# Vision transformer block with mixture of experts, one core: clock-holding products moved from the attention steps to the stretch before the token tiles, exp(min(x,0)) taken straight from PSUM, late weights loaded later

## What is computed

```python
h = concat([cls_tok, concat([cls_token, patches @ W_emb + b_emb]) + pos_embedding])
q, k, v = split(layernorm(h) @ qkv_w.T)          # 12 heads of 16
fmap(x) = elu(x) + 1                              # max(x, 0) + exp(min(x, 0))
out = wl * local_band(q, k, v, window 12) + ws * stride_band(q, k, v, 3) + wg * global_band(q, k, v, 12 anchors)
h = h + out @ out_w.T
xs = layernorm(h); topv, topi = top_k(softmax(xs @ Wg), 2); cw = topv / sum(topv)
h = h + sum over the 2 choices of cw * (relu(xs @ W1[e] + b1[e]) @ W2[e] + b2[e])     # 8 experts, 192 -> 768 -> 192
```

## Time and profile before

| | us |
|---|---|
| three runs | 254.42, 254.91, 259.94 (median 254.91) |
| the profiled execution | 253.24, of which its span is 251.3 |
| PE busy in the span | 226.0 (90%) |
| DVE, ACT, POOL busy | 141.4, 111.2, 71.6 |
| mean granted TensorE clock | 0.971 of full speed |

### The profile page before, as it was taken

The page is one execution under the profiler, slowest core; times in us unless marked ns, Lnnn a source line. Parts: engine busy times, 40 slices in busy tenths (PEclk is TensorE's granted clock), DMA queues, the critical chain, the costliest instruction groups (busy, mean ns, idle before and its releaser), DMA issues.

```text
span 251.3 us, 5038 instructions
## 1 busy us (share of the span) xinstructions
PE 226.0 (90%) x1662; PEld 193.5 (77%) x1662; DVE 141.4 (56%) x422; ACT 111.2 (44%) x253; POOL 71.6 (28%) x87
## 2 busy tenths in 40 slices
PE   8979998898999999999989839879999999999930
PEld 8968896675777757676878719679999999999930
DVE  5353588696859578574656790557867324334100
ACT  2364847753323744535086870345334344243210
POOL 4013160832040502213036610003324224233240
PEclk9999999999999999999999956999999999999996
DMA  6999999999500000001014945522423323322213
GB/s 129 199 239 160 232 265 267 301 259 265 194 4 0 3 1 4 0 0 31 0 32 144 329 95 132 118 78 49 73 40 57 55 37 60 54 39 18 28 18 90
DMA packets 26261, 25.78 MB, mean 103 GB/s; under 512 B 4970, under 2 KB 23261, under 8 KB 26221
## 3 DMA queue, kind: packets, MB, share of 16 engines
q1 hardware_dynamic: 22333, 22.17, 35.3%
q0 software_dynamic: 3568, 2.64, 7.9%
q10 hardware_dynamic: 336, 0.66, 1.5%
HBM read 16.57 MB, written 7.77 MB: 97 GB/s over the span
## 4 chain that ended last, share of the span: by engine, by line
PE 66%; DVE 10%; DMA 9%; ACT 7%; issue 4%; SPq 1%; POOL 1%; another core or an unknown queue 0%; DVEq 0%; POOLq 0%; ACTq 0%
PE ps L1025 11%; PE ps L1002 11%; PE ps L825 6%; PE ps L738 6%; PE ps L567 5%; DMA sums<-ys,xs 5%; DMA wemb<-in_L_tok_W_emb 4%; PE ps L1014 3%; PE ps L598 3%; PE ps L701 3%; PE ps L572 2%; PE ps L734 2%; PE ps L811 2%; ACT w1hi L1573 1%; ACT w1hi L1574 1%
## 5 line engine op out<-in xcount | busy, mean ns | idle before, releaser
L1765 POOL DMA_INDIRECT sums<-ys,xs x17 | 26.3, 1546 | 73.5 <-ACT ys L1652 66.8
L1025 PE MATMUL ps<-w2s,hidT 128*128 x204 | 36.1, 327 | 1.1 <-DVE hidT L1448 0.8
L567 PE MATMUL ps<-ones 114*128 114x128 f32 x238 | 34.8, 301 | 1.1 <-DVE ones L1073 1.1
L1025 PEld LDWEIGHTS ps<-w2s,hidT 128*128 128x128 f32 x204 | 33.1, 189 | 2.1 <-issue 1.6
L567 PEld LDWEIGHTS ps<-ones 114*128 114x128 f32 x238 | 32.1, 213 | 2.1 <-DVE ones L1073 1.1
L1002 PE MATMUL ps<-w1hi,xhi 128*128 x68 | 24.4, 359 | 2.6 <-issue 1.3
L1427 DVE TENSOR_TENSOR xlo<-ps,xhi 128x128 fp32r<-128x128 f32 x17 | 5.0, 292 | 35.8 <-ACT xend L1645 35.8
L1652 ACT ACTIVATE ys<-ps,xs 128x192 f32<-128x192 f32 x17 | 7.2, 421 | 39.9 <-PE ps L1025 37.6
L1534 ACT ACTIVATE qlb<-ps,cst 96x228 f32<-96x228 f32 (+1 forms) x36 | 12.1, 425 | 17.2 <-PE ps L772 17.1
L825 PE MATMUL ps<-qlb,kT 96*114 96x342 f32 (+1 forms) x48 | 18.0, 457 | 1.7 <-DVE at L1219 1.1
L1219 DVE TENSOR_TENSOR at<-ps,cst 114x342 f32<-114x342 f32 (+1 forms) x24 | 11.3, 471 | 8.7 <-PE ps L825 8.3
(11 more groups left out here) (202 smaller groups left out, 462.5 us busy)
## 6 DMA issues: line engine op xcount, KB each, us to landing
w2s<-in_L_ffn_W SPq DMA_DIRECT2D x8, 576.0 KB
sent<-blank SPq DMA_DIRECT2D x1, 3977.0 KB, 31.6
w1s<-in_L_ffn_W SPq DMA_DIRECT2D x4, 768.0 KB, 17.2
xs<-sent SPq DMA_DIRECT2D x17, 96.0 KB, 2.0
w1s<-in_L_ffn_W SPq DMA_DIRECT2D x4, 384.0 KB, 18.6
w1hi<-w1hi SPq DMA_DIRECT2D x8, 192.0 KB, 3.0
ximg<-in_x SPq DMA_DIRECT2D x12, 96.0 KB, 7.8
w1s<-in_L_ffn_b SPq DMA_DIRECT2D x1, 792.0 KB
```

What stands on the lines that cost most here:

```text
L567: pe.matmul(bank[:, 0:128], ones[:], ones[:], start=True, stop=True)
L1025: last = pe.matmul(ps[6 + j % 2][:, 0:D], hidT[:, k, :], of_expert(w2s[:, :, k, :], expert), start=(k == 0), stop=(k == FCH - 1))
L1765: po.indirect_dma_start(sums, bass.IndirectOffsetOnAxis(ap=xs[:, j % NS, D + TAIL + 1:].bitcast(U32), axis=0), ys[:, j % 2, :], None, comp ...
```

## The change

1. *Feature map.* A row of ones is added to the turned, normalised tokens (`xhT`) and to the query and key columns of the turned weights (`wT`), so that the projection gives x + 1 in the same two matmuls (97 rows in place of 96 in the first). ACT takes exp(x + 1 - 1) from PSUM, with the bias tile `minus`; DVE makes min(max(x + 1, 1), exp(x)), which is the same function. `qkmin` and its step on DVE go. Three small memsets are added at DVE's start.
2. *Products of ones.* In the steps, the 3 asides at `m` 1 and 3 stay in step 3 alone; 3 asides are put ahead of `through_anchors` in steps 6 and 7. Step 8 is as before. Of steps 9 and 10 the ones of the first part of step 9 stay; 1, 1 and 2 in step 9, 8 and 1 in step 10 and the 6 behind it go. Behind the counts stand 4; then, in place of 3 and 26, there are 4 once ACT has rounded 3 experts, 5 once it has rounded 5, 5 once it has rounded 6, and 6 once all scatters have landed.
3. *Late W2.* The loads of experts 4 to 7 move behind the stores of `first` on SP's queue, with a semaphore of their own (`w2_late`), for which PE waits at tile 5; at tile 1 it waits for experts 0 to 3 alone.
4. *ACT.* `combine_out(1)` moves ahead of the rounding of experts 4 and 5. `tokens_high` signals after its first instruction; the second (`xend`) reads the SBUF result of the first and has a semaphore of its own.
5. *DVE.* The six sums `first` come ahead of `tokens_low(0)` and `tokens_low(1)`.
6. *PE at the tiles.* Four register loads stand ahead of the first tile. The five products of a half are reordered, so that those that need `xend` and `xlo` come later, each with its own wait; `turn_tokens(1)` goes between the two halves of tile 0.

```diff
@@ SP
-                sp.dma_start(w2s[:, e], w2[e]...).then_inc(w2_in, 16)
+                sp.dma_start(w2s[:, e], w2[e]...).then_inc(w2_in if e < AHEAD else w2_late, 16)
...
             attention_over(sp)
-            for e in range(AHEAD, E):
-                load_w2(e)
...
                 sp.dma_start(sums[t0:t0 + n, :], first[0:n, g, :]).then_inc(sums_in, 16)
+            for e in range(AHEAD, E):
+                load_w2(e)
@@ PE, project_qkv
                 for i in range(2):
+                    rows = HALF + 1 - i
-                    last = pe.matmul(ps[2][0:n, 0:2 * D], xhT[:, i, t0:t0 + n], wT[:, i, 0:2 * D],
+                    last = pe.matmul(ps[2][0:n, 0:2 * D], xhT[0:rows, i, t0:t0 + n], wT[0:rows, i, 0:2 * D],
@@ PE, the steps
                 if 0 <= t - 3 < GROUPS:
+                    if GROUPS <= t < GROUPS + 2:
+                        hold_clock_aside(ps[5], 3)
                     through_anchors(t - 3)
...
-                        elif t < GROUPS + 2:
+                        elif t == 3:
                             hold_clock_aside(ps[5], 3)
...
-                    if m == 2 and t == GROUPS + 4:
-                        hold_clock(ps[3], 8)
...
-                if t >= GROUPS + 3:
-                    hold_clock(ps[3], 1)
                 if 0 <= t - 5 < GROUPS:
                     logits(t - 5)
-                if t == GROUPS + 3:
-                    hold_clock(ps[3], 1)
...
                 if t == GROUPS + 3:
-                    hold_clock(ps[3], 2)
                     places(GROUPS - 2)
...
-            hold_clock(ps[3], 6)
             places(GROUPS - 1)
...
+            hold_clock(ps[3], 4)
             output_biases(range(4))
             turn_combine(range(4, GROUPS))
-            hold_clock(ps[3], 3)
+            pe.wait_ge(ac_w1_high, 3)
+            hold_clock(ps[3], 4)
             output_biases(range(4, GROUPS))
-            hold_clock(ps[3], 26)
+            for e in (4, 5):
+                pe.wait_ge(ac_w1_high, e + 1)
+                hold_clock(ps[3], 5)
+            pe.wait_ge(sent_in, 16 * TOP * GROUPS)
+            hold_clock(ps[3], 6)
@@ PE, the tiles
+            for j in range(FIXED):
+                experts[j] = pe.value_load(own[0:1, j:j + 1], min_val=0, max_val=E - 1)
             pe.wait_ge(dv_count, 1)
             turn_tokens(0)
-            turn_tokens(1)
...
-                    hidden(j, experts[j])
+                    hidden(j, experts[j], 0)
+                    if j == 0:
+                        turn_tokens(1)
+                    hidden(j, experts[j], 1)
                 if j == 1:
-                    pe.wait_ge(w2_in, 16 * E)
+                    pe.wait_ge(w2_in, 16 * AHEAD)
+                if j == AHEAD + 1:
+                    pe.wait_ge(w2_late, 16 * (E - AHEAD))
@@ DVE, features
-                ve.tensor_scalar(qkmin[0:n, :], src, 0.0, None, ALU.min).then_inc(dv_min, 1)
...
-                link(ve.scalar_tensor_tensor(qtok[0:n, g % 2, :], src[:, 0:D], 0.0, qkexp[0:n, 0:D], ALU.max, ALU.add))
+                link(ve.scalar_tensor_tensor(qtok[0:n, g % 2, :], src[:, 0:D], 1.0, qkexp[0:n, 0:D], ALU.max, ALU.min))
@@ DVE, ahead of the tiles
+            for g in range(GROUPS):
+                first_sum(g)
             tokens_low(0)
             tokens_low(1)
-            for g in range(GROUPS):
...
@@ ACT
-                    ac.wait_ge(dv_min, t + 1)
+                    ac.wait_ge(pe_qk, t + 1)
...
-                    ac.activation(qkexp[0:n, :], qkmin[0:n, :], ACT.Exp).then_inc(ac_exp, 1)
+                    ac.activation(qkexp[0:n, :], ps[2][0:n, 0:2 * D], ACT.Exp, bias=minus[0:n, :]).then_inc(ac_exp, 1)
...
             weights_high(3)
+            combine_out(1)
             weights_high(4)
...
             weights_high(5)
-            combine_out(1)
```

More of the change, by code:

```diff
@@ L74 @@
 NS = 6
+FIXED = 4
 EPS_LN = 1e-5
@@ L233, in build @@
         sb = pool(attn)
-        qkmin = sb("qkmin", [GTOK, 2 * D])
         qkexp = sb("qkexp", [GTOK, 2 * D])
@@ L704, in project_qkv @@
                 for i in range(2):
-                    last = pe.matmul(ps[3][0:n, 0:D], xhT[:, i, t0:t0 + n], wT[:, i, 2 * D:3 * D],
+                    last = pe.matmul(ps[3][0:n, 0:D], xhT[0:HALF, i, t0:t0 + n], wT[0:HALF, i, 2 * D:3 * D],
                                      start=(i == 0), stop=(i == 1))
@@ L986, in of_expert, with hidden @@
                 return weights[:, bass.ds(expert, 1)].rearrange("p e f -> p (e f)")
-            def hidden(j, expert):
-                pe.wait_ge(ac_x_high, j + 1)
-                pe.wait_ge(dv_x_low, j + 1)
-                for c in range(2):
-                    if j >= 1:
-                        pe.wait_ge(dv_hidden if c else ac_hidden, j)
-                    cols = slice(c * PASS, (c + 1) * PASS)
-                    products = ((xhi[:, j % 2, 0, :], w1hi[:, :, 0, cols]),
-                                (xlo[:, j % 2, :], w1hi[:, :, 0, cols]),
-                                (xhi[:, j % 2, 0, :], w1lo[:, :, 0, cols]),
-                                (xhi[:, j % 2, 1, :], w1hi[:, :, 1, cols]),
-                                (xend[:, j % 2, :], w1lo[0:END, :, 1, cols]))
-                    for n, (xx, ww) in enumerate(products):
-                        last = pe.matmul(ps[2 + c][:, 0:PASS], xx, of_expert(ww, expert),
-                                         start=(n == 0), stop=(n == len(products) - 1))
-                    last.then_inc(pe_hidden, 1)
+            def hidden(j, expert, c):
+                if c == 0:
+                    pe.wait_ge(ac_x_high, j + 1)
+                if j >= 1:
+                    pe.wait_ge(dv_hidden if c else ac_hidden, j)
+                cols = slice(c * PASS, (c + 1) * PASS)
+                products = ((xhi[:, j % 2, 0, :], w1hi[:, :, 0, cols]),
+                            (xhi[:, j % 2, 0, :], w1lo[:, :, 0, cols]),
+                            (xend[:, j % 2, :], w1lo[0:END, :, 1, cols]),
+                            (xlo[:, j % 2, :], w1hi[:, :, 0, cols]),
+                            (xhi[:, j % 2, 1, :], w1hi[:, :, 1, cols]))
+                for n, (xx, ww) in enumerate(products):
+                    if c == 0 and n == 2:
+                        pe.wait_ge(ac_x_end, j + 1)
+                    if c == 0 and n == 3:
+                        pe.wait_ge(dv_x_low, j + 1)
+                    last = pe.matmul(ps[2 + c][:, 0:PASS], xx, of_expert(ww, expert),
+                                     start=(n == 0), stop=(n == len(products) - 1))
+                last.then_inc(pe_hidden, 1)
             def turn_hidden(j):
@@ L1042, in _ @@
                             pe.wait_ge(dup_in[batch], 16 * len(repeated))
-                    experts[j] = pe.value_load(own[0:1, j:j + 1], min_val=0, max_val=E - 1)
+                    if j >= FIXED:
+                        experts[j] = pe.value_load(own[0:1, j:j + 1], min_val=0, max_val=E - 1)
                 elif j < TILES:
```

41 lines of the change are left out of this document (24 added, 17 removed).

## The result

The forecast was 245.8 us. In the first measurement the changed kernel took 261.66 us (median of 259.27, 259.78, 263.55, 265.79) and the kernel before 257.43 (254.42, 254.91, 259.94, 261.31), with a ratio of 1.019 and a 95% interval of 1.013 to 1.025. Measured again in the experiments, six executions of the change had a median of 259.21 against 260.5 for eleven of before, with a ratio of 0.986 (0.979 to 0.992). All ratios here count only the executions of each kernel that lie within about 1.5% of its fastest. The two ratios disagree in sign, and one program's executions lie far apart: the 58 of before in the experiments between 253.57 and 283.09. Their time goes with the granted clock. Clocks of single executions are therefore given throughout. Over all, the change has a median of 259.6 (10 executions) and before 257.6 (58): no gain, where 9 us were forecast.

A forecast was written before the change was run, and what follows sets the result against it. PE was taken as the bound, partly with needless products of ones. Terms -1.2 - 3.2 - 2.7 - 1.0 - 1.0 = -9.1 made 245.8 us from a median of 254.91; own range 243 to 248.5, chance 0.48.

The forecast's parts named there:

- D, the clock falls within steps 4 to 7: Rival: without the asides, PE drops to half clock in the attention steps; 265 us, chance 0.05.
- Feature map, forecast -1.2: Projections of the first groups: dropping `qkmin` shortens DVE's chain until PE bounds from group 3; -1.2 us, bounds 0 and -3.4.
- one of the two gains of 0.6: Feature map: group 1 was to gain 0.6 us and group 2 another 0.6.
- Asides, forecast -3.2: Steps 4 to 7: asides out give -4.2 us, two added blocks cost 1.0; bounds -5.2 and +1.0.
- C: Rival: in the steps DVE takes the place of the asides, so their -4.2 is zero; 250.0 us, chance 0.12.
- Routing to tiles, forecast -2.7: Counts to token turn: PE's backlog at half clock ends at 156.0 instead of 158.66; bounds -0.5 and about -7.7.
- if the clock rises after 13 of them: Last 16 ones before the tiles, 32 records: full clock after 13 records makes them last 5.1 us, against 7.3 without.
- Register loads, forecast -1.0: Four loads moved ahead of tile 0 hide under PE's backlog, saving 1.0 us before tile 1; bounds 0, -1.0, or +1.5 unhidden.
- Start of tile 0, forecast -1.0: Token turn to first tile product: a shorter rounding cuts 1.68 us to 0.67, -1.0.
- Tiles, forecast even: Token tiles: PE bound by its own products, 4.57 us per tile, with no product added or removed.
- B, the clock back early: Rival: the clock holds or returns early before the tiles and scatters bound; first product 152.6, 241.8 us, chance 0.22.

The follow-up runs named there:

- f3: The change with three full products of ones added before the scores of m = 1 and 3 in steps 4 to 7; 253.9 us, ratio to before 0.993.
- h1: Same kernel as e1, run again on another chip; five of six executions at 250.58 to 252.25 us, one at 259.67.
- e4: The kernel before with the feature map of the change alone; 255.8 us, ratio to before 0.995.
- e1: The change with the narrow ones of steps 4 to 7 back as before, its own tail kept; 253.9 us with h1 included.
- g2: The change with the ones of steps 9 and 10 and the six behind them back, narrow ones still out; 263.8 us.
- e3: The change with the narrow ones of steps 4 to 7 and the ones of steps 9 and 10 back; 250.1 us with g4 included.
- g4: Same kernel as e3, run again on another chip; 244.86 to 250.29 us in six executions, ratio to before 0.967.
- e2: The kernel before with the change's edit of the narrow ones in the steps alone; 268.4 us with h2 included.
- h2: Same kernel as e2, run again on another chip; 268.4 us over both sets.
- g1: The change unedited, run again on a third chip; six executions from 250.9 to 268.16 us.
- h4: g2 with the narrow ones of step 6 back at m = 1 and 3; 256.0 us.
- f1: The kernel before with three full products of ones in place of the narrow ones in steps 4 to 7; 256.7 us.
- g3: f2 with the late W2 loads back at their old, early place; 249.6 us.
- f2: f3 with the ones of steps 9 and 10 and six behind them back, without narrow blocks ahead of steps 6 and 7; 252.0 us, ratio to before 0.979.

## Why the prediction was wrong, by its steps

**What failed: "D, the clock falls within steps 4 to 7", priced at 0.05.** It was the case that came, in all ten executions of the change: two profiles show it (101 to 132 and 101 to 133), and none of the ten lies above a clock of 0.927, while the changed tail alone leaves 0.955 (f3, h1). Its price of 265 was close to the first median of 261.66. The reason I gave against it, "PE without asides is still busy for nearly all of a step, and the granted clock shows no dip there at all", failed twice. A nearly busy PE did not keep the clock (8.85 of 10 us busy, then half). And "no dip at all" was one execution: 30 of 58 of before lie below 0.96, so that program lost its clock in about half of its executions already. What the prediction lacked was a price for PE's clock as it stands over many executions; the narrow ones were read as work that nobody needs, and they were part of what kept it up. The sign was in the times shown: 259.94 beside 254.42 and 254.91, 5 us that no row of the one profile explains. I read it as noise.

**The work itself was about right.** Less half clock, the change stands at 237.5 and before at 248.7: 11.2 us, give or take 3. The terms made 9.1, in which the forecast had some 6 us more half clock before the tiles than before (134 to 150 against 10.2), worth 2.3; so 11.4 is what to compare. The clock then took it back: a median of 55 us at half against 22, and 33 x 0.4 = 13. That the sum agrees so well is in part luck, since single terms missed:

**Feature map, forecast -1.2.** Mis-sized: it gave 0.7. The projections of groups 0, 1 and 2 (by PE's timeline; before, then the change):

```profile
26.31 1.52 PE L701 MATMUL ps<-wT,xhT 96*114 96x384 f32 x4
36.31 1.46 PE L701 MATMUL ps<-wT,xhT 96*114 96x384 f32 x4
44.56 1.52 PE L701 MATMUL ps<-wT,xhT 96*114 96x384 f32 x4
```

```profile
26.48 1.52 PE L706 MATMUL ps<-wT,xhT 97*114 97x384 f32 x4
36.47 1.46 PE L706 MATMUL ps<-wT,xhT 97*114 97x384 f32 x4
44.03 1.52 PE L706 MATMUL ps<-wT,xhT 97*114 97x384 f32 x4
```

From group 1 to group 2 are 8.25 before, 7.72 in e4 (37.32 to 45.04) and 7.56 in the change. Over all profiles it is 7.56 to 7.73 in the 13 with the new feature map and 8.25 to 8.87 in the five without. From group 0 to group 1 (9.99 to 11.00 with it, 9.99 to 10.31 without) and from group 2 to group 3 (14.0 either way) nothing is gained. So one of the two gains of 0.6 came, the other did not. As forecast, the 97th row cost nothing (1.52 either way), and the memsets ran in DVE's wait for the images.

**Asides, forecast -3.2.** Right to within the estimate, perhaps somewhat high. Steps 4 and 5 (from L796 to L796, L801 to L801 after) are 0.96 and 1.13 us shorter (13.30 against 14.26, and 13.93 without the added block against 15.06), as forecast at 0.8 to 1.1, with waits at the fourth score (0.74 and 0.35). In step 6 DVE was late by 1.15, a piece of C, and up to the fall the step gained 0.55 only (88.03 to 100.38 against 89.86 to 102.76). Less half clock: change against e1 and h1 -3.4, g2 against e3 and g4 -2.3, e2 and h2 against before -2.0.

**Routing to tiles, forecast -2.7.** From the last `project_out` to the token turn the change is 0.6 us shorter (29.0 against 29.6), h1 not at all. In the change the counts to the token turn took 16.2 us (151.4 to 167.6), forecast 14.4: "if the clock rises after 13 of them" failed, it rose just before the end, within 165 to 166. In h1, whose steps held, the clock did rise where forecast:

```profile
141.46 0.20 PE L962 MATMUL ps<-run,ones 114*1 114x8 f32 x2
150.56 5.54 PE L570 MATMUL ps<-ones 114*128 114x128 f32 x32
158.45 0.30 PE L982 MATMUL ps<-cst,xs 128*128 128x128 f32 x1 [2.35 <-issue]
```

Counts at 141.5 (forecast 141.6), ones over at 156.1 (forecast 156.0), and then a wait of 2.35 that I had priced only as a bound (+1.5 in place of -1.0).

**Register loads, forecast -1.0.** That 2.35 is theirs as far as the trace shows: they fill the time, and nothing else is waited for. The rows of h1 for the four ahead of the tiles, and for its other four, after the tiles have begun:

```profile
L1039 PEldq TENSOR_LOAD <-own x4: 497/799/1113, 153.7 to 156.9; - x4
L1051 PEldq TENSOR_LOAD <-own x4: 298/300/308, 176.7 to 190.6; - x4
```

(Least, median and greatest in ns, and when they started.) One takes 0.30 us later on, but 0.8 here, beside the copies of `w1hi` and the stores of `first`, which SP issues from 153.67 on. Beside the tile loads alone it stayed short: in g4, where the four started at 149.9 to 152.1, 0.31 at the median and 0.49 at most. PE stood bare behind its ones by 2.35 us in h1, 0.71 in the change, 0.51 in g4. The gain at the second tile was there: 3.4 us from tile 0's first product to tile 1's (168.69 to 172.06) against 4.5 (160.34 to 164.83).

**Start of tile 0, forecast -1.0:** turn to product 1.09 (167.60 to 168.69) against 1.84 (158.50 to 160.34), -0.75. **Tiles, forecast even:** right, 4.57 us each late in the run (232.88 to 237.45) as before. The late W2 was issued at 170 to 175 and did not hold tile 5 (PE waited for nothing there), but POOL's adds beside it did wait:

```profile
177.42 1.62 POOL L1785 DMA_INDIRECT sums<-ys,xs  x1 [22.55 <-ACT ys L1673]
183.60 2.21 POOL L1785 DMA_INDIRECT sums<-ys,xs  x1 [4.55 <-DMA sums<-ys,xs]
```

**B, the clock back early,** priced for 241.8, comes nearest in g4, which has the ones back that the change took out: half clock for 3 us before the tiles, and the first product at 153.94, where B had 152.6 (with shorter steps).

## What to carry to other kernels

Before taking out work that "nobody needs" from an engine whose granted clock can fall to half, look at the spread of the times and not at one profile: if some executions are several us above the others, the clock is lost now and then already, and what is removed there may be paid at 0.4 us for each us at half clock. Take such fillers out last, one place at a time, and take many executions of each. The ones in front of a stretch can matter more than those in it: here those of steps 9 and 10, which looked like waste, kept the half clock before the tiles to 7 us or less instead of 17 to 21. Register loads put in front of a loop can stand bare beside a burst of copies and stores; standing earlier they might not, which no run here tried.

## What the runs showed of the hardware

- One program's executions on one core of one chip differ by up to 29 us in 255 (254.4 to 283.1, beside g1), with the mean granted clock from 0.969 to 0.855. Nothing in the program differs. What decides it between executions was not found.
- PE at half clock and busy for all of 20 us (100 to 120) did not get its clock back; in h4 not in some 55 us, over 50 of which (120 to 170) it was busy all the time. The Trainium skill, page "TensorE: Matmul & The Clock Gate", section "Part 1: The HAM clock gate", has the clock follow how busy PE is. By busy time alone these stretches contradict it; they show the half clock lasting while PE is never idle by its busy time.
- Kernels with ones at both places of the steps kept the clock through the steps in about half of their executions (before 28 of 58, e3 and g4 7 of 10, e1 and h1 5 of 10, f1 7 of 12), without them in none (the change 0 of 10, e2 and h2 0 of 10, g2 0 of 6). In how often it fell, full, narrow or doubled ones made no difference that could be told. Why a missing 0.8 us in a nearly full engine matters so much stays open.
- The scatters had landed 4.7 (before) and 6.0 us (g3) after the end of their last issue beside 2.3 MB of weight loads, and after 2.7 without these (f2).
- A register load from SBUF took 0.30 us alone, 0.31 at the median beside the tile loads (g4), and 0.8 at the median and 1.11 at most beside the copies of `w1hi` and the stores of `first` (h1).
